# Two of four heads' softmax probabilities turned by VectorE and transfers, inverse sums applied to the value products

## The reference

```
h   = layernorm(x)
q   = h @ w_q;  k, v = ctx @ w_k, ctx @ w_v        # 16 heads of 64
a   = softmax(q k^T / 8) v                         # per batch and head, 256 x 256
x   = x + a @ w_o + b_o
h   = layernorm(x)
g   = softmax(h @ router_w + router_b)             # 8 experts, the 2 best, capacity 640
x   = x + sum over chosen experts of g_e * (gelu(h @ w1_e + b1_e) @ w2_e + b2_e)
```

## Time and profile before

| | |
|---|---|
| median of 3 runs | 995.42 us (994.77 to 996.41) |
| profiled execution | 993.48 us |
| its span | 991.4 us |
| mean granted TensorE clock | 0.991 of full speed |
| busy: PE, DVE, ACT, POOL | 97%, 79%, 63%, 28% of the span |
| DMA | 49057 packets, 56.77 MB |

### The profile page before, as it was taken

One profiled execution on the slowest core, in us unless ns is written; L12 is line 12 of the kernel. 1 busy time (PEld: TensorE's weight loads), 2 busy tenths in 40 slices (PEclk: granted clock), 3 DMA queues, 4 the chain that ended last, 5 costly groups with the idle time before them and its releaser, 6 DMA issues.

```text
span 991.4 us, 23339 instructions
## 1 busy us (share of the span) xinstructions
PE 964.9 (97%) x8434; PEld 876.0 (88%) x8434; DVE 781.9 (79%) x2095; ACT 622.3 (63%) x1740; POOL 281.8 (28%) x440
## 2 busy tenths in 40 slices
PE   8899999999999999999999999999899999999995
PEld 7778888888888888888888888888789999999995
DVE  6887778889898988888888988877987766677662
ACT  5777776777767776777777767776734433344420
POOL 5541121313142232313132241302433233321233
PEclk9999999999999999999999999999989999999998
DMA  8440101011010101011010101000242554344522
GB/s 245 133 133 2 33 1 34 23 34 55 2 54 13 36 14 34 13 33 45 2 44 6 33 9 33 17 1 16 87 136 82 134 140 95 73 124 130 137 28 27
DMA packets 49057, 56.77 MB, mean 57 GB/s; under 512 B 5948, under 2 KB 44842, under 8 KB 48816
## 3 DMA queue, kind: packets, MB, share of 16 engines
q1 hardware_dynamic: 40112, 46.30, 15.0%
q0 software_dynamic: 8832, 8.98, 5.6%
HBM read 36.01 MB, written 24.20 MB: 61 GB/s over the span
## 4 chain that ended last, share of the span: by engine, by line
PE 90%; DVE 5%; ACT 2%; DMA 1%; issue 1%; POOL 0%; POOLq 0%; SPq 0%; ACTq 0%; DVEq 0%
PE psum L613 24%; PE psum L710 12%; PE psum L882 11%; PE psum L696 10%; PE psum L680 10%; PE psum L864 10%; PE psum L727 9%; DVE prob L1146 2%; PE psum L838 1%; ACT prob L945 1%; PE psum L625 1%; PE psum L751 1%; PE psum L743 1%; DMA rows<-slot_table 1%; PE psum L805 1%
## 5 line engine op out<-in xcount | busy, mean ns | idle before, releaser
L945 ACT ACTIVATE prob<-psum,negmax 128x256 f32<-128x256 f32 x512 | 239.9, 488 | 88.5 <-DVE negmax L1135 88.5
L895 ACT ACTIVATE probt<-psum 128x512 f32<-128x512 f32 x256 | 158.1, 626 | 57.5 <-PE psum L696 57.5
L1135 DVE TENSOR_REDUCE negmax<-psum 128x2 f32<-128x512 f32 x256 | 159.8, 680 | 27.3 <-PE psum L680 27.1
L1146 DVE TENSOR_SCALAR prob<-prob,invtot 128x256 f32<-128x256 f32 x512 | 170.5, 396 | 4.5
L696 PE MATMUL psum<-ident,prob 128*128 128x128 f32 x1024 | 150.8, 274 | 1.6 <-DVE prob L1146 1.6
L1055 ACT ACTIVATE hid<-psum,b1t 128x640 f32<-128x640 f32 x64 | 50.9, 795 | 129.3 <-PE psum L864 129.3
L696 PEld LDWEIGHTS psum<-ident,prob 128*128 128x128 f32 x1024 | 120.1, 141 | 10.6 <-ACT probt L895 1.8
L710 PE MATMUL psum<-probt,v 128*64 128x256 f32 x1024 | 125.7, 388 | 0.0
L550 POOL DMA_INDIRECT slot_table<-row,picki x64 | 65.1, 1017 | 174.5 <-DVE picki L1307 148.9
L945 ACT ACTIVATION_READ_ACCUMULATOR prob<-psum,negmax 128x1 f32 x512 | 112.8, 220 | 0.0
L589 POOL DMA_INDIRECT out_rows<-y,rowi x40 | 65.1, 1628 | 165.5 <-DVE y L1366 159.5
(11 more groups left out here) (195 smaller groups left out, 2674.5 us busy)
## 6 DMA issues: line engine op xcount, KB each, us to landing
w1r<-in_w SPq DMA_DIRECT2D x8, 1024.0 KB, 7.9
w2r<-in_w SPq DMA_DIRECT2D x8, 1024.0 KB, 10.4
slot_table<-blank SPq DMA_DIRECT2D x8, 662.5 KB, 9.6
rows<-slot_table SPq DMA_DIRECT2D x7, 662.5 KB, 5.2
xin<-in_x SPq DMA_DIRECT2D x16, 256.0 KB, 2.9
out_rows<-x SPq DMA_DIRECT2D x16, 256.0 KB, 3.2
c<-in_ctxt SPq DMA_DIRECT2D x16, 128.0 KB, 3.1
c<-in_ctxt SPq DMA_DIRECT2D x32, 64.0 KB, 2.9
```

The source lines that it names most:

```text
L895: copy = lambda dst, src, **kw: act.activation(dst, src, ACT.Copy, **kw)
L945: last = act.activation(prob[:, m % 2, u, qb, :], psum[:, u, qb * S:(qb + 1) * S], ACT.Exp, bias=negmax[:, m % 2, u, qb:qb + 1], accum_out ...
L1135: dve.tensor_reduce(negmax[:, m % 2, u, :], psum[:, u, :].rearrange("p (q s) -> p q s", q=ST), AX.X, ALU.max, negate=True).then_inc(sem("m ...
L1146: last = dve.tensor_scalar(prob[:, m % 2, u, qb, :], prob[:, m % 2, u, qb, :], invtot[:, m % 2, u, qb:qb + 1], None, ALU.mult)
```

## The change

Period numbers in `MOVED` (6 to 61) treat heads 0 and 1 otherwise. `prob` is now laid out with the key half ahead of the query half. Once exp of a head is done, `square0` or `square1` (DVE) turns each 32x32 block of it in its place. `move(m)` (SP) then issues 16 transfers from `prob` to `probt`, one for each pair of a 32-partition group of the source and one of the destination; each moves 32 partitions x 8 pieces of 32 values (128 bytes). PE's `turn0`, `turn1` and ACT's `copy0`, `copy1` are left out in these periods; `pv(m)` on PE, and the next `exp` into the same buffer on ACT, wait for the transfers. Heads 2 and 3 are turned as before, and all four in the other periods.

`norm0` to `norm3` are gone in all periods. One `inv` (DVE) takes all inverses; `inv_out` (SP) writes them to memory as single values, `inv_in` (two transfers) reads them back, spread over 64 partitions each, into `invrows`; `a_norm` (DVE) multiplies the product of `pv` by them in PSUM, before `a_hi`. The turns wait for `exp` in place of `norm`.

SP's steps are now part of the list: in each period `inv_out` and `inv_in` of m - 1 and `move` of m, and `traffic` (loads of x and context, the store of x2) in every fourth. The clearing of `slot_table` is spread over periods 2 to 4. Within a period PE's, ACT's, DVE's, POOL's and SP's steps are now written one engine after the other, with pv right behind scores, and the router's, ln and x2 steps at other places. `xn` and `x2t` share one tile, so `ln1` and `x2t_sb` each wait for the other's reader.

```
+MOVED = range(6, PERIODS - 2)
+SQ = 32
+GROUPS = P // SQ
...
+def turned(m):
+    return (2, 3) if m in MOVED else (0, 1, 2, 3)
...
+        out += [("scores", m)] + ([("pv", m - 2)] if m >= 2 else [])
...
+            out += [("q", m + 1), ("turn2", m - 1), ("k", m + 1), ("turn3", m - 1), ("v", m)]
...
+        out += steps("exp0 exp1", m) + [("q_hi", m + 1)] + ([("a_hi", m - 2)] if m >= 2 else [])
...
+            out += [("copy2", m - 1), ("k_hi", m + 1), ("exp2", m), ("copy3", m - 1), ("exp3", m), ("v_sb", m)]
...
+        out += ([("split_lo", 5)] if m == 1 else []) + steps("max2 max3", m) + [("inv", m - 1)]
+        out += [("slot", b - 3)] if r == 2 and 3 <= b else []
+        out += [("a_norm", m - 2)] if m >= 2 else []
+        out += [("bias", b - 2)] if r == 3 and 2 <= b else []
+        out += [("square0", m)] if m in MOVED else []
+        out += [("ln1_stats", 1)] if m == 1 else []
+        out += [("q_lo", m + 1)] + ([("a_lo", m - 2)] if m >= 2 else []) + [("k_lo", m + 1)]
+        out += [("square1", m)] if m in MOVED else []
...
+        out += steps("inv_out inv_in", m - 1) + ([("move", m)] if m in MOVED else [])
+        out += {2: steps("clear", 0), 3: steps("clear", 1), 4: steps("clear", 2)}.get(m, [])
+        out += [("traffic", b - 2)] if r == 1 and 2 <= b else []
...
-        prob = sb(rest, "prob", [2, UNITS, ST, S])
+        prob = sb(rest, "prob", [2, UNITS, ST, ST, P])
...
+            def inv_out(m):
+                sp.wait_ge(sem("inv"), m + 1)
+                sp.dma_start(inv_table[m % 2].rearrange("u (q p) -> p u q", p=P), invtot[:, m % 2, :, :],
+                             allow_slow_non_contiguous=True)\
+                  .then_inc(sem("inv_out"), 16)
+
+            def inv_in(m):
+
+                sp.wait_ge(sem("inv_out"), 16 * (m + 1))
+                if m >= 1:
+                    sp.wait_ge(sem("a_norm"), m)
+                for h in range(2):
+                    sp.dma_start(invrows[h * HD:(h + 1) * HD, :, :],
+                                 inv_table[m % 2].rearrange("(c h) s -> h c s", h=2)[h].partition_broadcast(HD))\
+                      .then_inc(sem("inv_in"), 16)
+
+            def move(m):
+
+                sp.wait_ge(sem("square"), 2 * (m - MOVED[0] + 1))
+                sp.wait_ge(sem("pv"), m - 1)
+                for a in range(GROUPS):
+                    for g in range(GROUPS):
+                        sp.dma_start(
+                            probt[g * SQ:(g + 1) * SQ, m % 2, 0:2, :, :]
+                            .rearrange("p u k (q s) -> p (u k q) s", q=ST)[:, :, a * SQ:(a + 1) * SQ],
+                            prob[a * SQ:(a + 1) * SQ, m % 2, 0:2, :, :, :]
+                            .rearrange("p u k q s -> p (u k q) s")[:, :, g * SQ:(g + 1) * SQ])\
+                          .then_inc(sem(f"moved{m % 2}"), 16)
...
             def pv(m):
...
-                pe.wait_ge(sem("probt"), UNITS * (m + 1))
+                pe.wait_ge(sem("probt"), turns_to(m, UNITS - 1))
+                if m in MOVED:
+                    pe.wait_ge(sem(f"moved{m % 2}"), 16 * moves_to(m))
...
             def exps(m, u):
...
+                if m >= 2 and u in turned(m - 2):
+                    act.wait_ge(sem("turn"), turns_to(m - 2, u))
+                elif m >= 2:
+                    act.wait_ge(sem(f"moved{m % 2}"), 16 * moves_to(m - 2))
...
+            def a_norm(m):
+
+                dve.wait_ge(sem("pv"), m + 1)
+                dve.wait_ge(sem("inv_in"), 32 * (m + 1))
+                at = work_bank("pv", m).rearrange("p (c s) -> p c s", c=2)
+                dve.tensor_tensor(at, at, invrows[:, :, :], ALU.mult).then_inc(sem("a_norm"), 1)
+
+            def square(m, u):
+                dve.wait_ge(sem("exp"), UNITS * m + u + 1)
+                at = flat(prob[:, m % 2, u, :, :, :])
+                dve.transpose(at, at).then_inc(sem("square"), 1)
```

More of the change, by code:

```diff
@@ L57, with turns_to, moves_to @@
 assert CAP == ET * P and CAP % 2 == 0 and HALF <= 512
+MOVED = range(6, PERIODS - 2)
[3 more added lines that the diff above has]
+    return (2, 3) if m in MOVED else (0, 1, 2, 3)
+def turns_to(m, u):
+    return sum(len(turned(i)) for i in range(m)) + sum(h <= u for h in turned(m))
+def moves_to(m):
+    return GROUPS * GROUPS * len(range(MOVED[0] + (m - MOVED[0]) % 2, m + 1, 2))
 def timeline():
@@ L73, in timeline @@
             *steps("max2 max3", 0), ("split_hi", 4), *steps(k, 1), ("exp1", 0), ("split_lo", 4),
-            *steps("exp2 exp3 v v_sb", 0), ("split_hi", 5), *steps(half[0], 0)]
+            *steps("exp2 exp3 v v_sb", 0), ("split_hi", 5)]
     for m in range(1, PERIODS - 2):
         b, r = divmod(m, PER_B)
[L77 to L81, removed]
@@ L94, in timeline @@
[L94 to L102, removed]
@@ L103, in timeline @@
[L103 to L109, removed]
+        four = len(turned(m - 1)) == 4
+        out += [("scores", m)] + ([("pv", m - 2)] if m >= 2 else [])
+        out += [("logits", b - 2)] if r == 3 and 2 <= b else []
@@ L110, in timeline @@
+        if four:
+            out += [("q", m + 1), ("turn0", m - 1), ("k", m + 1), ("turn1", m - 1), ("v", m), ("turn2", m - 1)]
+        else:
+            out += [("q", m + 1), ("turn2", m - 1), ("k", m + 1), ("turn3", m - 1), ("v", m)]
         if r == (1 if b else 2) and b + 1 < B:
-            out += steps(xt, b + 1)
+            out += [("xt", b + 1)]
+        if r == 2 and 1 <= b:
+            out += [("o", ST * (b - 1))]
         if r == 2 and 2 <= b:
-            out += steps("x2t x2t_sb", b - 2)
@@ L114, in timeline @@
[L114 to L119, removed]
+            out += [("x2t", b - 2)]
         if r == 0 and 2 <= b:
             out += [("o", ST * (b - 2) + 1)]
-        out += steps("turn3 copy3", m - 1)
-        if r == 1 and 3 <= b:
-            out += [("pos", b - 3)]
+        out += [("turn3", m - 1)] if four else []
@@ new lines, in timeline @@
+        out += [("copy3", m - 1)] if four else []
+        out += [("gate_exp", b - 3)] if r == 0 and 3 <= b else []
+        out += [("x2t_sb", b - 2)] if r == 2 and 2 <= b else []
+        out += steps("max0 max1", m) + ([("x2add", ST * (b - 2) + 1)] if r == 1 and 2 <= b else [])
+        out += ([("split_lo", 5)] if m == 1 else []) + steps("max2 max3", m) + [("inv", m - 1)]
+        out += [("slot", b - 3)] if r == 2 and 3 <= b else []
+        out += [("a_norm", m - 2)] if m >= 2 else []
+        out += [("bias", b - 2)] if r == 3 and 2 <= b else []
@@ L150, in timeline @@
             ("pick", d)]
+    out += [*steps("inv_out inv_in", m - 1), ("load_w", 0), *steps("inv_out inv_in", m), ("inv_out", z),
+            ("traffic", d), ("inv_in", z), ("load_base", 0), ("traffic", e), ("load_w", 1)]
     out += [("iota", 0), ("scatter", c - 1), ("w_lo", 0), ("w_lo", 1), ("ln2_root", d), ("scatter", c),
```

174 lines of the change are left out of this document (98 added, 76 removed).

## The result

The changed kernel takes 1691.24 us (median of 4, 1685.28 to 1694.9) against 995.91 us before: a ratio of 1.698, 95% interval 1.694 to 1.702. Slower was forecast, but the size is more than five times the forecast's: 695 us in place of 125, outside the range of 1033 to 1226.

The account below looks back on a forecast made before the run. SP's queue was to bound periods 6 to 61: issues 10.35, landing 2.4 and traffic 0.65 make 13.4 us against 11.08, +130 us; with -5 for small edits, 993.5 becomes 1118.5, median 1120 us, range 1033 to 1226.

Parts of the forecast that it names:

- What bounds it: Periods 6 to 61: SP's in-order queue sets the period, 13.4 us (11.9 to 15.2) against 11.08, +130 us.
- The landing: SP's wait after inv_out until its 1024 4-byte values are in memory: 2.4 us, ends 2.0 and 3.2.
- The upper end of 15.2: Longest period forecast for SP's queue, in us, with the 3.2 landing and the 0.63 pitch.
- The pitch: Time per issue in SP's bursts of inv_in and move: 0.575 us, ends 0.516 and 0.63; 18 issues cost 10.35.
- The row at 7.59: Trace row of the starting burst (7.59 to 8.22), read as a 64-partition load with a pitch of 0.63 us.
- The eight other periods: Periods outside 6 to 61; the queue's cost was summed over 56 periods only.
- What PE gets back: Two heads' transposes no longer on PE: 1.18 us a period, 66 us in all, PE's period 9.90 us.
- The readers "two periods later": A value product waits for DVE before ACT may copy it, but its readers come two periods later.
- The added prices: DVE's a_norm and block turns at 0.69 us each, 128-byte packets at 14.8 ns, copies to probt down to 144.
- rival (b): DMA engines bind: 128-byte packets at 59 ns, 19.8 us a period, +490 us, 1480 us; chance 0.05.
- Rival (a): SP's queue keeps up at 0.42 us an issue and PE stays the bound: 934 or 924 us; chance 0.22.
- The small gains: Small edits: slow scalings at two places in the chain vanish, -5 us (0 to -10).

Follow-up runs that it names:

- the quick landing: Changed kernel with the inverses stored in 32-byte pieces (1216.32 us), or block-turned and stored as 128 rows of 128 bytes with the reference's output (1222.41 us).
- the three shown without any moves: Three stores in the run of the changed kernel where only period 61 is moved and inverses still go through memory; 1243.97 us (1.252).
- the fast kernel: Reordered run through memory (1000 us), with each period's four probability loads issued one period later, between the inverses' store and load; 970.17 us (0.976).

## Why the prediction was wrong

**What bounds it: right.** It named SP's queue as the bound and the sum of its round as the period. The chain (39% SP, 35% a landing that only SP waits for) shows this. With the quick landing the kernels take 1216 and 1222 us, just inside the forecast's range (to 1226). The landing is then near the forecast's 2.4 us (2.2 in the mean), and it is the issues that take the round to 15.2. The upper end of 15.2 had them otherwise, with a landing of 3.2, so that the two agree is in part luck.

**The landing: the step that failed.** "I take 2.4, between the two small ones; 2.0 and 3.2 are the ends." Measured from the store's issue to the load's: 10.5 us in the median of the changed kernel (8.2 to 14.9, mean 10.1), and 8.9 to 11.5 in the three shown without any moves. In the mean it costs 7.7 us a period more than taken. That is 430 us over 56 periods, and the run with 32-byte pieces puts it at 475. The bounding rows were two reads and a large store. None was a store of single 4-byte values. The Trainium skill (DMA: Bandwidth & Descriptors, Rules for kernel authors) says that a non-contiguous last dimension lowers to one descriptor for each element and should be rearranged. The trace agrees on the number: with pieces of 32 bytes the 64 stores have 57344 packets fewer, 896 each. The prediction counted the 1024 pieces and priced them by the packet, and the packets did pass quickly. The same page's 512 bytes (Specifications) does not separate the two: pieces of 32 and 128 bytes, also below it, landed within 1.7 us.

**The pitch: too low.** 0.575 was taken, 0.63 the end; measured 0.65, with a slow issue of 1.4 to 1.9 us in some of the bursts. On 18 issues the pitch is 1.4 us a period, and with the slow ones it is 1.8 us, 100 us over 56 periods. That it goes by the transfer and not by its pieces was right. The row at 7.59 was misread: by the kernel's text it is a load of 128 partitions, and the two of 64 partitions behind it go at 0.575 each. So the nearest shape in the trace gave just what was taken, and no row of the kernel before shows the 0.65 of a 32-partition transfer from place to place.

**The eight other periods: put at nothing.** The sum counted 56 periods, but the inverses travel in all 64. Landing and issues make the round 22.9 us in the mean of the periods 8 to 56, where 13.4 were forecast. From the maxima of period 6 to those of period 62 that is 507 of the missing 571 us, since the first and last of these periods are shorter. The other 64 are outside. There the changed kernel takes 59 us more than the one before, 18 ahead of period 6 and 41 from period 62 on, where the forecast had 5 less; without the inverses' transfers it takes 3 more.

**What PE gets back: read too high.** The 37.74 us of the turns count each instruction to its end, and PE starts the next product before that. The chain of the kernel before has the time that a turn really adds:

```profile
324.31 0.44 PE psum L696 x4
324.74 2.88 PE psum L727 x24
```

That is 0.44 us for a head's four and not 0.59, so 0.88 a period and 49 us in all, not 66, and PE's bound is 10.2 us and not 9.9. It changes nothing where SP's queue is the bound, but it is what the fast kernel must be held against: its 24 us are half of 49. Its periods take 10.61 us.

**The readers "two periods later": wrong.** `o` reads the value product late, but its work bank is wanted again in the same period, by k or v. The text named the ring of `prob` and not the ring of three banks. In the changed kernel this stood behind the landing; alone it costs 61 us, 36 of them by the order.

**The added prices: right.** A block turn takes 0.70 us (0.69 taken), a_norm 0.70 (0.69), and 144 copies to `probt` are left. A 128-byte packet took 12.2 ns in the mean (14.8 taken). DMA engines were no bound: 25.5% of them on this queue, and rival (b) never came near. Rival (a) fell too: no burst ran at 0.42. The Trainium skill's sentence that issue time is usually small beside the transfer did not hold here (DMA: Bandwidth & Descriptors, Issuing engines are not separate DMA queues): in the run with the moves alone an issue takes 0.61 of the 1.9 us to its landing, and 18 issues at 0.65 are 11.7 us, more than PE's period.

**The small gains** of 5 us were not measured apart.

**Open.** What makes the landing of the 4-byte store long was not settled: the number of pieces (1024 against 128), their size, or that neighbouring values of one line come from different partitions. The run with 32-byte pieces changed all three. That its packets pass and then 8 us go by is seen in the trace, but not why.

## What to carry to other kernels

Price a transfer that somebody waits for by its landing, and take that from a row of the same piece size and direction; where no such row exists, the price is unknown, and a bound from other shapes is none. If a queue waits for a landing, put transfers behind the waited one that need nothing of it: the same work took 1042 us in one order of the engines' and SP's queues and 970 in another. Read what a step costs an engine from the chain or from the start of the next step, not from the sum of busy times, where steps overlap. And where a step is put into the way of a product, ask who wants the bank it lies in, not only who reads it.

## What was not expected of the hardware

A store of 1024 values of 4 bytes to memory released its waiter 8.2 to 14.9 us after its issue (median 10.5), the same 4 KB in 128 pieces of 32 bytes after 1.7 us (median). SP's DMA queue carried no packet for the last 5.6 to 9.4 us of it (median 7.8). Transfers between places on the chip, 32 partitions each, have an issue pitch of 0.65 us with 256 pieces and 0.64 with 128. Loads from memory of 1024 pieces of 128 bytes each land in 2.9 us (median).
